# Five steps moved in the written-out order of an attention-and-experts kernel on one core

## The reference

```python
x = x + attention(layernorm(x))        # x: 32 batches of 256 tokens, width 128, fp32
x = x + experts(layernorm(x))

def attention(x):                      # 16 heads of 8
    q, k, v = split(x @ w_qkv.T)
    s = q @ k.T * 8 ** -0.5
    s = s - max(s)                     # stablemax: a cubic of s - max, not exp
    p = 1 / (1 - s * (1 - 0.5 * s * (1 - s / 3)))
    return (p / sum(p)) @ v @ w_out.T + b_out

def experts(x):                        # 4 experts, hidden 512, the best 2 weighted
    h = silu(x @ w1) * (x @ w3)
    return sum(gate * (h @ w2))
```

## Time and profile before

| | |
|---|---|
| median of 3 runs | 1118.57 us |
| runs | 1117.99 to 1120.09 us |
| profiled execution, its own time | 1117.78 us |
| its span | 1116.0 us |
| TensorE granted clock, mean | 0.998 |
| busy: TensorE matmul / weight load | 98% / 83% |
| busy: VectorE, ScalarE, GpSimd | 86%, 89%, 67% |

### The profile page before, as it was taken

How to read it: one execution, slowest core, us unless ns; L and a number is a source line. 1 busy time by engine, 2 the same in 40 slices (tenths; PEclk the granted TensorE clock), 3 DMA queues, 4 the chain that set the end, 5 groups by cost and what they waited for, 6 DMA issues and landing times.

```text
span 1116.0 us, 29087 instructions
## 1 busy us (share of the span) xinstructions
PE 1093.2 (98%) x9940; PEld 931.1 (83%) x9940; DVE 963.7 (86%) x1667; ACT 993.5 (89%) x1035; POOL 742.9 (67%) x936
## 2 busy tenths in 40 slices
PE   6889999999999999999999999999999999999998
PEld 5668888888888888888888888888888888888888
DVE  5889888899888899988889988889988889998844
ACT  1989999999999999999999999999999999999982
POOL 5357676687776677776677767668776667776530
PEclk9999999999999999999999999999999999999999
DMA  6343433323433223343333343322344322334100
GB/s 192 112 144 123 125 116 100 96 89 122 124 123 107 89 88 111 123 128 111 96 92 96 122 124 119 102 90 84 122 124 128 108 91 93 105 120 125 31 6 11
DMA packets 130445, 117.49 MB, mean 105 GB/s; under 512 B 15810, under 2 KB 125026, under 8 KB 130402
## 3 DMA queue, kind: packets, MB, share of 16 engines
q1 hardware_dynamic: 128066, 113.78, 33.2%
q10 hardware_dynamic: 2336, 3.15, 0.9%
HBM read 94.18 MB, written 21.09 MB: 103 GB/s over the span
## 4 chain that ended last, share of the span: by engine, by line
PE 93%; DVE 2%; DMA 1%; ACT 1%; ACTq 1%; SPq 1%; issue 0%; DVEq 0%
PE banks L1337 33%; PE banks L1632 21%; PE sc L1433 11%; PE banks L1355 11%; PE sc L1615 4%; PE misc L1337 2%; PE misc L1469 2%; DVE mx L1019 2%; PE banks L1666 2%; PE misc L1491 1%; PE misc L1442 1%; PE banks L1615 1%; PE sc L1337 1%; PE sc L1820 1%; PE misc L1684 1%; PE banks L1331 1%
## 5 line engine op out<-in xcount | busy, mean ns | idle before, releaser
L501 POOL TENSOR_TENSOR hid<-hid,gate_all 128x512 f32<-128x512 f32 x240 | 380.7, 1624 | 161.9 <-DMA gate_all<-gate_scratch 154.5
L932 DVE SCALAR_TENSOR_TENSOR poly<-w_sq,sc 128x1024 f32<-128x1024 f32 x251 | 303.0, 1218 | 38.4 <-ACT w_sq L684 32.3
L684 ACT ACTIVATE w_sq<-sc 128x1024 f32<-128x1024 f32 x251 | 254.9, 1030 | 37.2 <-PE sc L1433 33.5
L1337 PE MATMUL banks<-xn_hi,w_hi 128*128 128x256 f32 x976 | 286.4, 293 | 0.0
L1337 PE MATMUL banks<-xn_lo,w_hi 128*128 128x256 f32 x976 | 275.3, 282 | 0.0
L1337 PE MATMUL banks<-xn_hi,w_lo 128*128 128x256 f32 x976 | 274.3, 281 | 0.0
L1632 PE MATMUL banks<-w_sb,hid 128*128 128x128 f32 x1920 | 250.5, 281 | 0.4 <-DVE hid L924 0.4
L796 ACT ACTIVATE poly<-poly 128x2048 f32<-128x2048 f32 x128 | 240.3, 1899 | 0.3
L1632 PEld LDWEIGHTS banks<-w_sb,hid 128*128 128x128 f32 x1920 | 225.6, 191 | 16.4 <-DVE hid L924 0.9
L801 ACT ACTIVATE poly<-poly 128x2048 f32<-128x2048 f32 x128 | 236.8, 1896 | 0.0
L1019 DVE TENSOR_REDUCE mx<-sc 128x4 f32<-128x1024 f32 x192 | 229.4, 1211 | 5.5 <-PE sc L1615 5.0
(11 more groups left out here) (192 smaller groups left out, 1334.6 us busy)
## 6 DMA issues: line engine op xcount, KB each, us to landing
qk_scratch<-qk_split SPq DMA_DIRECT2D x32, 512.0 KB, 3.1
q_pad<-qk_scratch SPq DMA_DIRECT2D x256, 64.0 KB
k_tile<-qk_scratch SPq DMA_DIRECT2D x124, 128.0 KB, 2.6
q_tile<-qk_scratch SPq DMA_DIRECT2D x124, 128.0 KB, 2.6
k_stack<-qk_scratch SPq DMA_DIRECT2D x124, 128.0 KB
gate_all<-gate_scratch SPq DMA_DIRECT2D x30, 512.0 KB, 4.4
x_in<-in_L_attn_x_dram SPq DMA_DIRECT2D x32, 128.0 KB, 2.1
x_res<-in_L_attn_x_dram SPq DMA_DIRECT2D x32, 128.0 KB, 2.3
```

Source lines behind the costliest of these rows:

```text
L501: nc.gpsimd.tensor_tensor(h, h, by_token.unsqueeze(1).to_broadcast([128, 2, C, 128]), ALU.mult).then_inc(gated, 1)
L684: nc.scalar.activation(w_sq[:, u % 2, :], distance_buf(n, u), ACT.Square).then_inc(sq_ok, 1)
L932: nc.vector.scalar_tensor_tensor(poly[:, u, :], w_sq[:, u % 2, :], 3.0, distance_buf(n, u), ALU.add, ALU.mult).then_inc(poly_ok, 1)
L1337: last = nc.tensor.matmul(dst, lhs[a], rhs[b], start=(k == 0), stop=(k == len(terms) - 1))
```

## The change

Five steps move; nothing is added or removed, and no wait is written anew.

- ScalarE, first half: the copy of attention's transpose goes from behind square(6) to behind square(7), so silu(6) and square(7) come ahead of it.
- ScalarE, second half: the third Exp goes ahead of the fourth Ln, so the fourth Exp follows directly on the fourth Ln.
- VectorE, first half: polynomial(4) goes ahead of hidden(3).
- TensorE, first half: distance(4) goes ahead of `values_T`.
- TensorE, second half: score(1) goes from behind down(0, 1) to behind down(0, 2).

```diff
@@ ScalarE, first half @@
                     square(6)
-                    attention_T_copied()
                     silu(6)
                     square(7)
+                    attention_T_copied()
                     silu(7)
@@ ScalarE, second half @@
                     weights_of(1)
+                    weights_of(2)
                     log_of(3)
-                    weights_of(2)
                     weights_of(3)
@@ VectorE, first half @@
                     normalized()
+                    polynomial(4)
                     hidden(3)
-                    polynomial(4)
@@ TensorE, first half @@
                     up_b_unit(i, off - 2, 3)
+                    distance(4)
                     values_T()
-                    distance(4)
                     up_a_unit(i, off - 2, 4)
@@ TensorE, second half @@
                     down(0, 1)
+                    down(0, 2)
                     score(1)
-                    down(0, 2)
                     down(0, 3)
```

More of the change, by code:

```diff
@@ L1512, in first_half @@
                     up_b_unit(i, off - 2, 2)
+                    up_b_unit(i, off - 2, 3)
                     up_a_unit(i, off - 2, 3)
-                    up_b_unit(i, off - 2, 3)
+                    distance(4)
                     values_T()
-                    distance(4)
                     up_a_unit(i, off - 2, 4)
```

## The result

| | before | after |
|---|---|---|
| median, 12 runs each | 1118.76 us | 1121.34 us |
| lowest and highest run | 1117.60 to 1120.09 | 1119.99 to 1123.05 |
| ratio of the two, 95% interval | | 1.0021 [1.0013, 1.0029] |
| profiled execution: its own time, span | 1117.78, 1116.0 | 1120.46, 1118.7 |
| mean period | 33.069 us | 33.152 us |

The change costs 2.6 us, 0.21%: slower, by as much as was forecast (1121.2 us). The mean period is the distance from the first weight load of the values projection (L1469) to the next one, over the same 24 settled periods; it is 0.083 us longer. It comes from one execution of each kernel, so a difference of 0.01 us in it says nothing.

A forecast was written before the change was run, and what follows sets the result against it. TensorE was taken as the bound, held up at up_a(6) by silu(5) and at router_logits by VectorE's experts_added. 30 x 0.085 = 2.55, plus 0.13, 2.7 us on 1118.57, gave 1121.2 us; range 1117.8 to 1124.0.

The forecast's parts named there:

- The term of the sum: First half: hidden(3), now behind polynomial(4), ends later and holds silu(5), and so up_a(6), 0.085 us in each of 30 periods.
- this case: Slower as worked out: 0.085 to 0.13 us a period, 1121 to 1122.7 us, chance 0.48.
- The first wait of the prediction: Second half: TensorE's router_logits waits for experts_added on VectorE, so a later output projection delays TensorE's return.
- Each link: First half: reciprocal to polynomial(4) 0.79 us, on to hidden(3) 1.13, hidden(3)'s end to silu(5) 0.10; up_a(6) shifts with silu(5).
- The two kinds of period: Settled periods of two lengths, forecast at 33.05 and 33.25 us after the change.
- The removed wait at distance(6): TensorE, first half: distance(6) no longer waits for polynomial(4); no gain, as silu(5)'s wait covers it; faster rival 0.07.
- The three moves costed at nothing: Attention's transpose copy, third Exp and score(1): no cost, except 0.13 us once in the last period for the Exp.
- ScalarE's cover: silu(1) waits 0.28 us for TensorE, which was to take up the 0.13 us lost at the fourth Exp.
- The rival that had it gone: The fourth Exp's 0.13 us reaches the path, 3.9 us more: 1125.1 us with the first case, 1122.6 alone; chance 0.11.
- The dependent Exp: ScalarE, second half: the fourth Exp, directly behind its Ln, loses 0.10 + 0.03 = 0.13 us.
- the estimate of 0.09: The same Exp's wait by the Trainium skill's overlap figure alone: 0.09 us, 30 of them 2.8 us.
- U: Experiments' rival theory: the overlooked up-projection swap makes up_a(4) wait for silu(3), 0.06 to 0.07 us a period; no chance given.

The follow-up runs named there:

- e11: Kernel before with the output projection ahead of down(0, 0) and VectorE's last maximum ahead of the copy of the queries' transpose; 1116.23 us, ratio 0.9978.
- e9: Changed kernel without the overlooked swap of up_b(3) and up_a(3), with three SiLU buffers instead of two; 1117.78 us, ratio 0.9993 to the kernel before.
- e4: Kernel before with only distance(4) moved ahead of values_T on TensorE; 1125.46 us, ratio 1.0054.
- e5: Kernel before with only the moves of attention's transpose copy, the third Exp and score(1); 1118.97 us, ratio 1.0000.
- e8: Kernel before with each of ScalarE's four second-half Exp directly behind its own Ln; 1121.95 us, ratio 1.0027.
- e2: Changed kernel with the overlooked swap of up_b(3) and up_a(3) undone, leaving the five moves; 1121.28 us, ratio 1.0021 to the kernel before.
- e6: Changed kernel with polynomial(4) put back behind hidden(3) on VectorE; 1124.40 us, ratio 1.0055 to the kernel before.

## Why the prediction was right, and where it wasn't

- **The term of the sum held.** silu(5) held by hidden(3) was forecast at 0.085 us a period. Without the edit that the forecast had left out, the period grows by 0.076, and by 0.087 over the same kernel with the hold removed. 30 x 0.083 = 2.5 us, and 0.14 in the last period, make the 2.6 us of the medians. That the medians meet the forecast to 0.1 us is luck: the interval of the ratio spans 1.5 to 3.2 us. The lengths of the periods are the better evidence. The margin was thin too, and the chance given to this case was 0.48.
- **The first wait of the prediction was read too long.** router_logits stands idle for 0.24 us, but when nothing on VectorE holds it any more (e11) it still does so for 0.20. The sum did not use the 0.24, only that a later output projection comes through to TensorE, and that held.
- **Each link held to 0.01 us**: reciprocal to polynomial(4), polynomial(4) to hidden(3), the end of hidden(3) to silu(5), silu(5) to up_a(6). The margin that decided between no change and slower was 0.09 us in a chain of six steps; rows of one trace carried it, since each step is a queue's own spacing and repeats in every period. The two kinds of period came out at 33.07 and 33.24 us, where 33.05 and 33.25 were forecast.
- **The removed wait at distance(6) brought nothing**, as said, but the reason given was half of it. That it lay inside silu(5)'s wait is true of TensorE. By way of square(6) and polynomial(6) it also stood in VectorE's chain to down(0, 0), which in the kernel before was as long as TensorE's. Taking it off shortened one of two equal chains, and by little: in e9 distance(6) loads 0.14 us earlier than in the kernel before, but hidden(6) starts only 0.03 earlier. e4, which lengthens that chain, costs 0.21.
- **The three moves costed at nothing cost nothing** (e5). score(1): the third maximum starts without a wait. ScalarE's cover held: silu(1) still waits 0.20 for TensorE. The rival that had it gone needed more than those 0.28; four dependent pairs (e8) reach the path, one doesn't.
- **The dependent Exp lost 0.13**, as the rows had given, and not the estimate of 0.09. The Trainium skill (ScalarE: Activation LUTs, What ACT_TABLE_LOAD costs) has activations in a row overlap by about 93 ns. The trace agrees with that, 0.10. A dependent pair loses this overlap and 0.04 on top, from the end of the Ln to the start of the Exp.
- **A step of the working failed: the reading of the change.** The prediction took TensorE's up projections as unmoved, and they were not. The swap alone costs 0.034 to 0.043 us a period. It was luck that this did not spoil the number: silu(5) waits for the later of two delays; with three SiLU buffers the same oversight would have been a forecast of no change against a measured 1.0013.
- **A test of the prediction failed too.** "The forecast is wrong if silu(5) still names TensorE": it does name TensorE, and the forecast isn't wrong. A releaser's name is no test where two conditions end within 0.04 us. In e2, where they lie 0.10 apart, the name is right. The distance from the last weight load was the better test, and could have been written down from rows 6 and 7.

## What to carry to other kernels

A wait taken off an engine is worth nothing when a second wait right behind it ends later, and the swap that takes it off may lengthen the second: follow both to the same instruction and compare the ends. Moves of one producer and its consumer on two engines belong together, and half of a pair can cost several times the pair; test them in both halves before calling either good or bad. Where an order is held by a buffer's reuse, as silu(5) by hidden(3), one more buffer tells in one run whether that hold is the cost; run the old order with that buffer too. And an idle time ahead of an instruction isn't what its wait is worth: a part of it may stay when the wait is gone.

## What the runs showed that I had not expected

- The profile's releaser was wrong for silu(5) in two kernels, once in each direction: in the changed kernel it names TensorE, where VectorE ended 0.04 us later, and in e9 VectorE, where TensorE ended last. The totals of the waits inherit this: 27 waits on hidden products in the changed kernel and 56 in e2, though hidden(3) holds silu(5) in both.
- Two chains on different engines ended within about 0.01 us of each other at down(0, 0) in the kernel before, and neither is named in its waits, since TensorE has no gap there long enough to be listed. e4 and e6, which lengthen one of them, make it show (0.21 <-DVE hid L924), and so does e8 in every second period.
- Four dependent Ln and Exp pairs in a period take about 0.5 us of ScalarE and cost 0.096, on an engine that is busy for 89% of the span.
- The swap of up_a(3) and up_b(3) starts silu(3) about 0.7 us later and costs 0.034 to 0.043 us: the transposes and distance(4) still lie between up_a(3) and up_a(4). U had expected about twice that; where the other half goes stays open.
